# A decoder layer on one Trainium2 core: GpSimd pre-adds of the softmax sums, four output buffers and a later inversion in cross-attention, and quantising one batch ahead in the output projection

## What is computed

```python
out = fq_floor(fq_floor(out) @ fq_round(w_out))          # self-attention, last line
...
q = (query @ Wq + bq)...; k = ...; v = ...               # cross-attention, (B, 16 heads, 512, 32)
attn = jnp.einsum('bhqd,bhkd->bhqk', q, k) * scale
attn = jnp.clip(attn, -CLAMP, CLAMP)
attn = jax.nn.softmax(attn, axis=-1)
x = jnp.einsum('bhqk,bhkd->bqhd', attn, v).reshape(B, Nq, Cq)
return x @ Wo + bo
```

## Time and profile before

| | us |
|---|---|
| median of three runs | 3699.03 |
| the profiled execution | 3686.1 |
| its span | 3684.1 |
| TensorE busy | 2770.5 (75%) |
| VectorE busy | 2544.9 (69%) |
| ScalarE busy | 1455.5 (40%) |
| GpSimd busy | 143.2 (4%) |
| stage 8, output projection, about | 1540 to 1689 |
| stage 10, cross-attention, about | 2038 to 2882 |

### The profile page before, as it was taken

One profiled execution on the slowest core, in us unless ns is written; L12 is line 12 of the kernel. 1 busy time (PEld: TensorE's weight loads), 2 busy tenths in 40 slices (PEclk: granted clock), 3 DMA queues, 4 the chain that ended last, 5 costly groups with the idle time before them and its releaser, 6 DMA issues. The chain is left out here.

```text
span 3684.1 us, 46619 instructions
## 1 busy us (share of the span) xinstructions
PE 2770.5 (75%) x13113; PEld 1055.1 (29%) x13160; DVE 2544.9 (69%) x4626; ACT 1455.5 (40%) x2397; POOL 143.2 (4%) x146
## 2 busy tenths in 40 slices
PE   1189999677775666556999677777777965999998
PEld 1134322111113334323444111111111333444443
DVE  6877799998997999743555565656556686455444
ACT  0000444499998999611222233333333101212221
POOL 0000333000000000000000000000000000000000
PEclk7599999555558999977999788888889977999999
DMA  5221231333324444354553322222223631001000
GB/s 200 73 91 46 92 117 76 110 125 121 121 106 130 137 145 148 126 194 164 193 183 130 89 76 64 73 68 65 76 62 117 229 124 32 23 23 36 33 23 23
DMA packets 209163, 374.66 MB, mean 102 GB/s; under 512 B 33689, under 2 KB 119705, under 8 KB 196625
## 3 DMA queue, kind: packets, MB, share of 16 engines
q1 hardware_dynamic: 204832, 356.46, 29.3%
q10 hardware_dynamic: 4208, 16.78, 1.2%
HBM read 217.48 MB, written 155.68 MB: 101 GB/s over the span
## 5 line engine op out<-in xcount | busy, mean ns | idle before, releaser
L1344 DVE TENSOR_REDUCE stats<-bank 128x1024 f32 (+1 forms) x352 | 408.0, 1216 | 64.8 <-PE bank L806 32.0
L1201 ACT ACTIVATE arena<-arena,scale 128x512 bf16<-128x512 int8 x512 | 408.2, 810 | 53.4 <-DVE arena L1539 53.4
L1657 DVE TENSOR_REDUCE arena<-bank 128x2 f32<-128x1024 f32 x256 | 311.7, 1218 | 148.8 <-PE bank L976 141.4
L866 PE MATMUL bank<-arena 64*128 64x512 bf16 x512 | 306.5, 605 | 104.8 <-DVE arena L1532 66.6
L1220 ACT ACTIVATE arena<-arena,scale 128x512 f32<-128x512 int8 x512 | 367.0, 802 | 12.9 <-DMA arena<-dq_scr 12.9
L1532 DVE CUSTOM_DVE_ANT_0 arena<-bank,arena,fac 128x512 int8<-128x512 f32 x512 | 349.6, 746 | 23.6 <-PE bank L866 11.4
L1288 ACT ACTIVATE arena<-bank 128x1024 f32<-128x1024 f32 x256 | 248.0, 1022 | 282.5 <-PE bank L992 282.5
L1020 PE MATMUL bank<-arena 128*32 128x512 f32 x2048 | 295.7, 657 | 0.0
L806 PE MATMUL bank<-arena 128*128 128x512 bf16 x1001 | 242.8, 384 | 62.7 <-DVE arena L1474 52.4
L1322 ACT ACTIVATE arena<-bank,arena,fac 128x512 f32<-128x512 f32 x128 | 99.5, 777 | 456.5 <-PE bank L1144 456.5
L976 PE MATMUL bank<-arena 128*128 128x512 f16 x512 | 180.3, 439 | 100.5 <-DVE arena L1657 86.7
(11 more groups left out here) (191 smaller groups left out, 3558.3 us busy)
## 6 DMA issues: line engine op xcount, KB each, us to landing
dq_scr<-arena SPq DMA_DIRECT2D x128, 256.0 KB, 2.0
arena<-dq_scr SPq DMA_DIRECT2D x128, 256.0 KB, 2.8
arena<-half_scr SPq DMA_DIRECT2D x256, 128.0 KB, 2.8
qkv_scr<-arena SPq DMA_DIRECT2D x8, 3072.0 KB, 9.7
arena<-in_x SPq DMA_DIRECT2D x16, 1024.0 KB, 7.1
arena<-qkv_scr SPq DMA_DIRECT2D x128, 128.0 KB, 2.2
o_scr<-arena SPq DMA_DIRECT2D x64, 256.0 KB, 3.0
arena<-o_scr SPq DMA_DIRECT2D x8, 2048.0 KB, 9.2
```

The lines of the kernel that those rows point to most:

```text
L866: return mm(dst, qE[r, h // 2, P * t:P * t + P], kE[r, h // 2, :], start=True, stop=True)
L1201: last = A(e_dump[:, NT * (h % 2) + t, :], dq8[:, h % 4, t, :], ACT.Exp, bias=negm_b[:, par, c:c + 1], scale=scale[:, S_DOTS:S_DOTS + 1], ...
L1344: return V.tensor_reduce(dst, src, ax, ALU.max, apply_absolute_value=True)
L1657: V.tensor_reduce(mxX[:, mp, hs, 2 * u:2 * u + 2], bank[:, 0:2, :], AX.X, ALU.max).then_inc(S("sX_red"), 1)
```

## The change

It makes six edits.

1. Four `oX` buffers in place of two; `values_out` waits for the store of the group four before.
2. `invert` of group i - 2 stands at the end of group i (c = 3, u = 1) instead of behind its first two reductions.
3. GpSimd adds the exponentials of key tiles 0 and 1, and of 2 and 3, for each of the four heads (`add_tiles`, 8 products of 128x512 f32 per group, into a new buffer `eS`), and TensorE's sums take two steps over `eS` (`sums_of`) instead of four over `eT`. The sums' second half moves to c = 2 of the next group; the value products move to c = 0, 1, 1 and 2.
4. The first ten score pairs of the stage rotate over banks 0 to 5 and may run two ahead of the reductions.
5. In the output projection VectorE quantises batch b + 1 before it takes the peak of batch b.
6. Two semaphore names are merged into one (`hC_in`, `hqD_in` to `h_in`), and ScalarE's loop is unrolled by four instead of two.

```diff
+START_AT = tuple((0, 2, 4)[n % 3] for n in range(2 * LEAD))
...
-        oX = cX(F32, 2, T)
+        oX = cX(F32, 4, T)
+        eS = cX(F32, 2, G, T)
...
+            def add_tiles(i, par, k):
+                pool.wait_ge(S("clipped"), i * 8 + 4 * k + 4)
+                if not (isinstance(i, int) and i == 0):
+                    pool.wait_ge(S("sumX_mm"), i)
+                hold(pool)
+                for g in range(G):
+                    nc.gpsimd.tensor_tensor(eS[:, k, g, :], eT[:, par, g, 2 * k, :], eT[:, par, g, 2 * k + 1, :], ALU.add
+                                            ).then_inc(S("eS_ready"), 1)
+
+            def group(i, r):
+                if not (isinstance(i, int) and i == 0):
+                    add_tiles(i - 1, (r + 1) % 2, 1)
+                if not (isinstance(i, int) and i < 3):
+                    divide(i - 3, (r + 1) % 4)
+                add_tiles(i, r % 2, 0)
...
-                if not (isinstance(h, int) and h == 0 and u == 0):
-                    pe.wait_ge(S("sX_red"), h * 2 + u)
+                if not (isinstance(h, int) and h * 2 + u <= free):
+                    pe.wait_ge(S("sX_red"), h * 2 + u - free)
...
+            def sums_of(i, par, k):
+                if k == 0:
+                    pe.wait_ge(S("nmT_ready"), i + 1 if isinstance(i, int) and i == GROUPS - 1 else i + 2)
+                pe.wait_ge(S("eS_ready"), i * 8 + 4 * k + 4)
+                hold(pe)
+                for g in range(G):
+                    last = mm(bank[XD * g:XD * g + XD, 7, :], ones, eS[:, k, g, :], start=k == 0, stop=k == 1)
+                if k:
+                    last.then_inc(S("sumX_mm"), 1)
...
+                for c_, half_, body in ((0, 0, lambda: sums_of(i, par, 0)), (0, 1, lambda: values_of(i, par, 0)),
+                                        (1, 0, lambda: values_of(i, par, 1)), (1, 1, lambda: values_of(i, par, 2)),
+                                        (2, 0, lambda: sums_of(i, par, 1)), (2, 1, lambda: values_of(i, par, 3))):
...
-                if not (isinstance(i, int) and i < 2):
-                    act.wait_ge(S(f"oX_stored{par}"), i * 8 - 8 * par)
-                A(oX[:, par, :], bank[:, 6, :], ACT.Copy).then_inc(S("oX_evac"), 1)
+                if not (isinstance(i, int) and i < 4):
+                    act.wait_ge(S(f"oX_stored{r % 2}"), (i - 2) * 8 - 8 * (r % 2))
+                A(oX[:, r, :], bank[:, 6, :], ACT.Copy).then_inc(S("oX_evac"), 1)
...
             def quantise_o(b, par):
                 dve.wait_ge(S(f"oH_in{par}"), b * 8 + 16 - 8 * par)
+                if not is_batch(b, 0):
+                    dve.wait_ge(S("ob_ready"), b)
...
-                dve.wait_ge(S("y_evac"), b * NT + 8 + NT)
-                amax(stats[:, bass.ds(b, 1)], yH[:, par], AX.XY).then_inc(S("y_peak"), 1)
-            batches(dve, quantise_o)
+                if not is_batch(b, 0):
+                    peak_y(b - 1, 1 - par)
+            through(dve, quantise_o)
+            peak_y(NB - 1, 1)
...
-                        if (c, u) == (0, 1) and not (isinstance(i, int) and i < 2):
+                        if (c, u) == (3, 1) and not (isinstance(i, int) and i < 2):
                             invert(i - 2)
```

More of the change, by code:

```diff
@@ L765, in _, with divide @@
             barrier(pool, 9)
-            def divide(i, par):
+            def divide(i, r):
+                par = r % 2
                 pool.wait_ge(S(f"rec_in{par}"), (i * 8 + 16 - 8 * par) * G)
@@ L770, in divide @@
                 hold(pool)
[L771 to L774, removed]
+                nc.gpsimd.tensor_tensor(oX[:, r, :], oX[:, r, :], recB[:, par, :], ALU.mult).then_inc(S("oX_ready"), 1)
+            def add_tiles(i, par, k):
[12 more added lines that the diff above has]
+                add_tiles(i, r % 2, 0)
+            for i in range(4):
+                group(i, i)
+            with pool.Fori(1, GROUPS // 4) as j:
+                for r in range(4):
+                    group(j * 4 + r, r)
+            add_tiles(GROUPS - 1, 1, 1)
+            divide(GROUPS - 3, (GROUPS - 3) % 4)
             barrier(pool, 10)
@@ L1018, in values_of, with products @@
                 for g in range(G):
-                    w = ones if k < 2 else vX[:, par, c, XD * g:XD * g + XD]
-                    last = mm(bank[XD * g:XD * g + XD, 7 if k < 2 else 6, :], w, eT[:, par, g, c, :],
+                    last = mm(bank[XD * g:XD * g + XD, 6, :], vX[:, par, c, XD * g:XD * g + XD], eT[:, par, g, c, :],
                               start=c == 0, stop=c == NT - 1)
                 if c == NT - 1:
-                    last.then_inc(S("sumX_mm" if k == 1 else "pvX_mm"), 1)
+                    last.then_inc(S("pvX_mm"), 1)
+            def products(i, par, c, half):
+                for c_, half_, body in ((0, 0, lambda: sums_of(i, par, 0)), (0, 1, lambda: values_of(i, par, 0)),
+                                        (1, 0, lambda: values_of(i, par, 1)), (1, 1, lambda: values_of(i, par, 2)),
+                                        (2, 0, lambda: sums_of(i, par, 1)), (2, 1, lambda: values_of(i, par, 3))):
+                    if (c, half) == (c_, half_):
+                        body()
             def group(i, r):
@@ L1034, in group @@
                     if previous:
-                        values_of(i - 1, (r + 1) % 2, c, 0)
+                        products(i - 1, (r + 1) % 2, c, 0)
                     if c == NT - 1 and not (isinstance(i, int) and i == GROUPS - 1):
@@ L1043, in group @@
                     if previous:
-                        values_of(i - 1, (r + 1) % 2, c, 1)
+                        products(i - 1, (r + 1) % 2, c, 1)
             for h in range(LEAD):
@@ L1059, in _ @@
                 for half in (0, 1):
-                    values_of(GROUPS - 1, 1, k, half)
+                    products(GROUPS - 1, 1, k, half)
             barrier(pe, 10)
@@ L1280, in group @@
                     if c == 0 and not (isinstance(i, int) and i < 2):
-                        values_out(i - 2, r)
+                        values_out(i - 2, (r + 2) % 4)
                     if c == 2 and not (isinstance(i, int) and i == 0):
-                        sums_out(i - 1, 1 - r)
+                        sums_out(i - 1, (r + 1) % 2)
                     if c == NT - 1 and not (isinstance(i, int) and i == GROUPS - 1):
-                        max_turned(i + 1, 1 - r)
+                        max_turned(i + 1, (r + 1) % 2)
                     for a in (0, 1):
                         act.wait_ge(S("sT_mm"), i * 8 + 2 * c + a + 1)
-                        A(eT[:, r, 2 * a:2 * a + 2, c, :], bank[:, 2 + 2 * a:4 + 2 * a, :], ACT.Exp,
+                        A(eT[:, r % 2, 2 * a:2 * a + 2, c, :], bank[:, 2 + 2 * a:4 + 2 * a, :], ACT.Exp,
                           scale=XSCALE / HALF ** 2).then_inc(S("eX_done"), 1)
             max_turned(0, 0)
-            for i in range(2):
+            for i in range(4):
                 group(i, i)
-            with act.Fori(1, GROUPS // 2 - 1) as j:
-                for r in range(2):
-                    group(j * 2 + r, r)
-            for i in (GROUPS - 2, GROUPS - 1):
-                group(i, i % 2)
-            values_out(GROUPS - 2, 0)
+            with act.Fori(1, GROUPS // 4 - 1) as j:
+                for r in range(4):
+                    group(j * 4 + r, r)
+            for i in range(GROUPS - 4, GROUPS):
+                group(i, i % 4)
+            values_out(GROUPS - 2, 2)
             sums_out(GROUPS - 1, 1)
-            values_out(GROUPS - 1, 1)
+            values_out(GROUPS - 1, 3)
             barrier(act, 10)
```

44 lines of the change are left out of this document (22 added, 22 removed).

## The result

| | before | after |
|---|---|---|
| median, us | 3696.47 (3693.9 to 3699.72) | 3601.89 (3598.7 to 3606.23) |
| ratio to before, 95% interval | | 0.9744 (0.9728 to 0.9761) |
| the profiled execution, us | 3686.1 | 3598.7 |
| its span, us | 3684.1 | 3596.9 |

The change makes the kernel 95 us faster by the medians, 87 us by the two profiled executions. The median before is that of four executions here; the forecast was made from three of them (3699.03). The forecast was 3635 us, with 3505 to 3705 as its range.

The account below looks back on a forecast made before the run. No engine was full; two overlapping waits, VectorE's reciprocals and ScalarE's output copy, with what followed cost 7.6 us per group. Savings 51 + 9 - 4 + 8 = 64 us took 3686.1 to 3622, plus 12.9 for the median: 3635, range 3505 to 3705.

Parts of the forecast that it names:

- The walk through a group: Cross-attention: reduction starts stepped through one group with GpSimd's additions; next group at 22.7 us, before any clock cost.
- The rule from two overlaps: GpSimd and VectorE reading SBUF take turns, one instruction at a time; an overlapped clip or product took about 0.55 us longer.
- the upper bound for the small instructions: VectorE's split of the maxima: each small instruction waits a full addition, period 22.7 us; without waits 19.9.
- Rival 1: Cross-attention: small VectorE instructions pass GpSimd unhindered, clock stays at 2.4 GHz; period 19.9, 3511 us; chance 0.20.
- rival 2: Cross-attention: GpSimd's four additions keep the port as one block, clock falls; period 28.4, 3757 us; chance 0.13.
- Rival 3: Cross-attention: the stall only changes place, reciprocals' loads arriving late for GpSimd's product; period about 25.75, 3680 us; chance 0.12.
- The clock: TensorE, idle 4.1 us before the turned maxima, may drop to its lower clock: 1.5 us per group, bounds 0 and 3.0.
- 29 periods: Cross-attention groups 1 to 30: period falls from 25.95 to 24.2 us, 51 us less in all.
- start of the stage: Cross-attention's first eleven reductions: three pairs of banks let them follow at 1.2 instead of 2.35 us, about 9 us less.
- end of the stage: Cross-attention's end: last additions and a later sum stand before the last reciprocals, adding 4 us (bounds 2 and 8).
- output projection: Batch period stays 16.8 us, load behind the store; one overlap gained at the end, 8 us less (bounds 3 and 16).
- TensorE's fewer sums: TensorE loses two of eight sum steps per group, 2.1 us; booked at nothing, VectorE's critical gap not being behind a sum.

Follow-up runs that it names:

- no_rotate: Kernel after with the first score pairs on the same two banks at every pair, as before the change: 3612.8 us, ratio 0.9766 to before.
- no_adds: Kernel after without GpSimd's additions, TensorE making the sums in four steps again, all else as changed: 3457.59 us, ratio 0.9356 to before.
- load_first: Kernel after with SyncE's load of batch b + 2 ahead of the store of batch b in the output projection: 3550.73 us, ratio 0.9605 to before.
- adds_01: Kernel after with GpSimd adding only key tiles 0 and 1, beside the split of the maxima; TensorE sums tiles 2 and 3: 3587.3 us.
- adds_23: Kernel after with GpSimd adding only key tiles 2 and 3, beside the clips; TensorE sums tiles 0 and 1: 3524.76 us.
- half_adds: Kernel after with each GpSimd addition over 256 of the 512 columns, half of each sum left out: 3526.63 us, ratio 0.9544 to before.
- adds_wait: Kernel after with the second four additions held until the next group's maxima are split: 3630.86 us, ratio 0.9827 to before.

## Why the prediction held

**The walk through a group** said 7.0, 9.1, 12.5, 16.9, 20.2 and 22.7 us for the fourth to the eighth reduction and the next group. The means of 29 groups of the kernel after are 7.3, 9.2, 12.5, 16.7, 20.8 and 23.2. The rule from two overlaps, that GpSimd and VectorE take turns instruction by instruction, carried this. So did the upper bound for the small instructions, which was a choice: no row before the change showed one that met GpSimd. They do wait, though two of the three and not each. The first starts just as an addition ends (L1712, 0.17 us at 2411.53). Rival 1, small ones unhindered, is refuted by their rows, and rival 2, four additions as one block, by the clip of 1.65 us between them and the two of 1.13 and 1.21. Rival 3 too: the loads of the reciprocals end GpSimd's idle time for 12.8 us in all.

For what contends the Trainium skill, "SBUF — State Buffer", section "Who interferes with whom", had named casts and tensor_scalar, and its row now exists: a cast of 16 elements per partition took 1.15 us on average beside the additions and 0.20 without. It also says that a reduction never contends on this chip, and the reductions here average 1.215 us, as without additions. For instructions with two inputs the page is narrower than the prediction put it: both inputs must lie in SBUF, and GpSimd must be reading SBUF too, as it does here. The page speaks of the pair of ports as held for an instruction; that the two engines alternate when GpSimd has four queued is what the rows show, and no block of four was seen.

**The clock** was put at 1.5 us per group within bounds of 0 and 3.0, and this period of 24.2 is the step that was off: the measured one is 23.2. The clock does fall in nearly every group, as said, but for some 3 us around the turn. What it costs can be read from the reductions' intervals: from the seventh to the eighth 4.1 us where the walk had 3.3, and 0.3 more up to the fourth, behind the first sum at half pace (1.69 us at 2397.29 where 1.06 is usual), together 1.1. The walk itself was 0.6 too long from the fourth reduction to the seventh, having three small instructions wait instead of two. Of the 1.0 us the clock makes 0.4 and the walk the rest. **The mis-sized term** is therefore the period: 29 us of the 33 by which the forecast was too high are 29 times this 1.0.

**The sum**, term by term, in us of the profiled executions:

| term | said | measured |
|---|---|---|
| 29 periods | -51 | -80 (752.7 to 672.7) |
| start of the stage | -9 | -9.8 (23.75 to 13.99, and no_rotate gives it back) |
| end of the stage | +4 (2 to 8) | +8.3 (from group 30's first reduction to the end of VectorE's last product with reciprocals: 42.4 to 50.8) |
| output projection | -8 | -7.1 (143.1 to 136.0, from its first load to the last peak's end) |
| together | -64 | -88.6 |

The spans differ by 87.2; the stage before the output projection ended 2.1 us later, which no term covers. The end of the stage came out just above its upper bound: in the last split a third small instruction waits too (1.17 us), and the additions go on behind the last scores. One part has a row of its own: GpSimd's last product stands behind its last four additions, and VectorE's first product with reciprocals, which had no wait before, waits 3.3 us for it (VectorE timeline of after):

```profile
2788.57 0.69 DVE L1772 TENSOR_TENSOR arena<-arena 128x512 f32<-128x512 f32 x1 [3.29 <-POOL arena L774]
```

How the rest divides was not tried. The 12.9 us that I added to reach the median were 10.4 for the kernel before and 3.2 for the kernel after.

**TensorE's fewer sums** were booked at nothing. No run isolates them: no_adds makes all of them and has the shorter period by 4.5 us, which is the additions' cost less whatever the fewer sums gave.

**The output projection** went as reasoned. The peaks are 16.8 to 17.0 us apart (the first two at 1567.38 and 1584.27), as before, because the load stands behind a store that waits for the peak; load_first shows that this order held back another 51 us.

What stays open: why the additions of one pair and of the other cost 197 us apart and 144 together. The doubled step of sums in both kernels is about 26 of these 53 us by the estimate above. The clock may explain some of the rest (adds_01 has its low level in every group already, so the second pair can't lose it again), but no run separates that from the shared waits.

## What to carry to other kernels

Work moved to GpSimd is priced by what VectorE does beside it, and not by the load it takes off another engine: a chain of instructions of 0.2 us each, on which TensorE waits, was the costliest neighbour here, since each can wait for nearly a whole addition of 1.23. Sparing TensorE two steps of 1.06 us, where it wasn't the bound, cost 144 us net. And when two waits overlap, the shorter one's cure shows nothing until the longer one is gone; here four buffers alone left the period as it was, and gave 100 us once the inversion had been moved.

## What the runs showed of the hardware that was not expected

A VectorE instruction of 16 elements per partition takes up to 1.21 us when it meets GpSimd's additions, and then goes on. GpSimd's additions of 128x512 f32 take 1.23 us each back to back (4.94 for four).

TensorE's granted clock stayed at 1.00 from 2100 to 2600 in no_adds and adds_23, where the wait for the maxima is 1.2 and 2.0 us a group, and was 0.89 to 0.91 in after, adds_01 and half_adds, where it is 3.8, 4.2 and 3.3. In these a longer wait cost not only itself but the pace of what came behind it. The length of this one wait doesn't tell the clock by itself: adds_wait has 0.85 with 65.4/32 = 2.0 us, and TensorE stands there a second time in each group, 2.53 us ahead of the sum at 2417.90.
